# The band mask of local attention: from a TensorE product to a ScalarE copy into PSUM, in five of eight slots

## What is computed

```
sim  = einsum('bhwie,bhwje->bhwij', bq, bk2) * 8
mask = (it < jb) | (it > jb + w) | (jb == -1)
sim  = where(mask, -max, sim)
out  = einsum('bhwij,bhwje->bhwie', softmax(sim), bv2)
```

## Time and profile before

| | |
|---|---|
| median of 3 runs | 3702.38 us (3701.47 to 3703.31) |
| profiled execution: its time, its span | 3697.9 us, 3695.9 us |
| PE busy | 3358.6 us (91%) |
| DVE busy | 2839.3 us (77%) |
| ACT busy | 2300.3 us (62%) |
| POOL busy | 2304.4 us (62%) |
| mean granted clock of TensorE | 0.960 |

### The profile page before, as it was taken

The page is one execution under the profiler, slowest core; times in us unless marked ns, Lnnn a source line. Parts: engine busy times, 40 slices in busy tenths (PEclk is TensorE's granted clock), DMA queues, the critical chain, the costliest instruction groups (busy, mean ns, idle before and its releaser), DMA issues. The chain is left out here.

```text
span 3695.9 us, 150639 instructions
## 1 busy us (share of the span) xinstructions
PE 3358.6 (91%) x64970; PEld 2462.3 (67%) x64970; DVE 2839.3 (77%) x3892; ACT 2300.3 (62%) x4617; POOL 2304.4 (62%) x2078
## 2 busy tenths in 40 slices
PE   7949999999999989999989999999999989999995
PEld 3736667666676666766666666766667666666663
DVE  5348778778878878878878878878878877887783
ACT  4326666666666666666666666666666666666664
POOL 0037666666766666766766766766666666676671
PEclk9769999999999999999999999999999999999997
DMA  1021111111111111111111111101111111111112
GB/s 31 18 75 35 32 30 32 29 30 61 32 30 31 32 30 58 33 32 29 33 29 61 32 29 31 33 28 60 32 29 32 32 29 57 34 32 29 29 32 71
DMA packets 94830, 133.99 MB, mean 36 GB/s; under 512 B 21065, under 2 KB 45152, under 8 KB 93280
## 3 DMA queue, kind: packets, MB, share of 16 engines
q1 hardware_dynamic: 86508, 123.78, 11.3%
q10 hardware_dynamic: 7668, 0.50, 0.2%
HBM read 25.60 MB, written 4.26 MB: 8 GB/s over the span
## 5 line engine op out<-in xcount | busy, mean ns | idle before, releaser
L1032 POOL TENSOR_TENSOR qs<-rprod 128x512 f32<-128x512 f32 x768 | 994.3, 1303 | 669.1 <-DVE rprod L1102 644.3
L1102 DVE TENSOR_TENSOR rprod<-ps,tab 128x1024 f32<-128x1024 f32 x768 | 929.5, 1218 | 284.8 <-PE ps L779 175.6
L1043 POOL TENSOR_TENSOR qs<-qs,rr 128x512 f32<-128x512 f32 x768 | 784.8, 1043 | 281.2 <-ACT rr L964 280.4
L777 PE MATMUL ps<-wh,xls 128*128 128x512 f32 x1152 | 548.3, 476 | 59.4 <-PEq L733 39.9
L828 PEld LDWEIGHTS ps<-pt,v 64*64 64x64 f32 x24768 | 398.6, 135 | 193.6 <-issue 97.0
L788 PE MATMUL ps<-con,qs 128*128 128x128 f32 x3080 | 508.3, 288 | 2.8 <-issue 2.8
L945 ACT ACTIVATE sq<-ps 128x512 f32<-128x512 f32 x384 | 228.6, 595 | 442.6 <-PE ps L779 438.0
L828 PE MATMUL ps<-pt,v 64*64 64x32 f32 x24768 | 442.1, 221 | 66.2 <-ACT pt L954 62.1
L1048 POOL TENSOR_TENSOR pr<-pr,rinv 128x512 f32<-128x512 f32 x386 | 420.1, 1088 | 127.4 <-DVE rinv L1143 127.4
L1121 DVE TENSOR_REDUCE ssq<-sq 128x16 f32<-128x1024 f32 x384 | 464.0, 1208 | 0.0
L779 PE MATMUL ps<-wh,xhs 128*128 128x512 f32 x1152 | 455.9, 396 | 0.0
(11 more groups left out here) (160 smaller groups left out, 5170.2 us busy)
## 6 DMA issues: line engine op xcount, KB each, us to landing
v<-v SPq DMA_DIRECT2D x384, 192.0 KB
v<-v SPq DMA_DIRECT2D x288, 64.0 KB
raw<-in_L_ffn_Wqkv SPq DMA_DIRECT2D x7, 1536.0 KB, 6.4
wo<-in_L_ffn_Wo SPq DMA_DIRECT2D x6, 512.0 KB, 8.6
sT<-so SPq DMA_DIRECT2D x22, 96.0 KB, 1.6
bias<-in_L_attn_hidden_states SPq DMA_DIRECT2D x8, 256.0 KB, 5.5
srow<-sT SPq DMA_DIRECT2D x8, 256.0 KB, 3.2
xrow<-in_L_attn_hidden_states SPq DMA_DIRECT2D x8, 256.0 KB, 4.1
```

The source lines that it names most:

```text
L777: nc.tensor.matmul(dst, al, bh, start=True, stop=False)
L1032: nc.gpsimd.tensor_tensor(qs[:, i % 2, j].rearrange("p (h s d) -> p h s d", s=2, d=HALF), prod[:, 0, j].rearrange("p (h s d) -> p h s d", ...
L1043: nc.gpsimd.tensor_tensor(q3, q3, rr[:, 8 * j:8 * j + 8].unsqueeze(2).broadcast_to([P, 8, DH]), ALU.mult).then_inc(cur["mul"], 1)
L1102: return nc.vector.tensor_tensor(prod[:, :, j, :].rearrange("p c (h d) -> p c h d", d=DH), ps[:, bank, :].rearrange("p (h d) -> p h d", d= ...
```

## The change

In full rounds, for the scores of slots 2 to 6, TensorE no longer forms the mask product. ScalarE copies the mask (bf16 in SBUF) into the score bank at the end of the slot before, that is at the end of slots 1 to 5, behind its copy `kT` and ahead of that slot's extra steps. The new event `mk` tells TensorE that it is there. The score products add to it as before. The scores of slots 7, 0 and 1 keep the product, because the bank SC is used by the feed-forward part between slots 7 and 1.

```diff
-                after(pe, "sub", i)
-                if i == 0 and pb0 is not None:
-                    pe.wait_ge(other["gl"], 3)
-                if i == 1 and pb0 is not None:
-                    pe.wait_ge(cur["h"], 3)
-                nc.tensor.matmul(ps[:, SC, :], identb[:], maskb[:, int(tb > 0), :], start=True, stop=False,
-                                 skip_group_check=True)
+                if full and 2 <= i <= 6:
+                    pe.wait_ge(cur["mk"], i - 1)
+                else:
+                    after(pe, "sub", i)
+                    if i == 0 and pb0 is not None:
+                        pe.wait_ge(other["gl"], 3)
+                    if i == 1 and pb0 is not None:
+                        pe.wait_ge(cur["h"], 3)
+                    nc.tensor.matmul(ps[:, SC, :], identb[:], maskb[:, int(tb > 0), :], start=True, stop=False,
+                                     skip_group_check=True)
                 after(pe, "qte", i)
                 after(pe, "kte", i)
...
+                if full and 1 <= i <= 5:
+                    act.wait_ge(cur["sub"], i + 1)
+                    nc.scalar.copy(ps[:, SC, :], maskb[:, int(unit(i + 1, 2)[1] > 0), :]).then_inc(cur["mk"], 1)
                 if i == 1 and nb is not None:
                     shift_high(nb, 1 - k).then_inc(cur["xh"], 1)
```

More of the change, by code:

```diff
@@ L190 @@
          "woa wo mean var gup aup w2 xh xl fq fr fh gl h x2 x1 fx fc fn fl "
-         "wh wl w1h w1l vc tab shifted cleared").split()
+         "wh wl w1h w1l vc tab mk shifted cleared").split()
 def chunked_attention(nc, t, ctx, sb0, sem0, clear, con, ident, ps, xT, sT):
```

## The result

Over 17 runs of each kernel the changed one takes 3716.46 us (median, 3705.25 to 3737.5) and the one before 3702.33 (3688.94 to 3713.05). The ratio is 1.0038, with a 95% interval of 1.0027 to 1.0049: slower by 10 to 18 us. The profiled execution of the changed kernel took 3705.25 us, with a span of 3703.4 and a mean granted clock of 0.962; 3697.9 and 0.960 stood against it before. Whole executions of one kernel scatter by 24 to 32 us, so most of what follows is read from the inside of a round, where most steps repeat to 0.01 us.

A forecast was written before the change was run, and what follows sets the result against it. TensorE bounds slots 1 to 3, VectorE and POOL slots 4 and 5, ScalarE the second rotation of slot 6. Gains 17.8 us, costs 31.5 us: +13.7 on 3697.9, plus 4.5 to the median: 3716, range 3700 to 3730.

The forecast's parts named there:

- The product is worth 0.22, not 0.31: TensorE's scores: removing a mask product saves 0.22 us; the remaining 0.09 is the switch to small pieces, which stays.
- It pays in slots 2 and 3 only: Plain rounds: removed products gain 0.22 us each in slots 2 and 3, and 0 in slots 4, 5 and 6.
- The reason given for slot 4: Slots 4 and 5: the residual can come earlier, but slot 5's gs still waits for POOL's chain; gain 0.
- Slot 5's copy costs its full length: End of slot 5, plain rounds: the copy stands before the square that times everything, moving the round's gate by 0.50 us.
- Rival 1: End of slot 5: the copy is hidden after all; -1.8 us, 3700.6, no change; chance 0.10.
- rival 3: TensorE's work is the limit throughout: 3650 if all five removed products pay, 3671 if only slots 2 to 4; chance 0.08.
- The copies in slots 1 to 4 of plain rounds are hidden: End of slots 1 to 4: ScalarE waits for TensorE's keys, 1.47 us before slot 5, so copies cost nothing.
- The rounds at a layer's change: new_hf0: two 0.50 us copies, two 0.22 gains; new_hf1: two copies, no gain; new_ff: two copies, slot 2's gain only.
- Copies stand ahead of the first two: 2 x 0.50: new_hf0, 6 rounds: copies ahead of the weight casts of slots 4 and 5, awaited by VectorE, cost 0.50 us each.
- The first round was put at two gains and no cost: First round: two removed products counted as gains of 0.22 us each, with no copy counted as a cost.
- TensorE's wait at slot 6's turn at about 0.95: Slot 6's turn: profile sign that TensorE's idle time, 0.51 us before, becomes about 0.95.
- rival 4: Slots 6 and 7: longer TensorE idling lowers the clock more often; another 8 such rounds make +20 us, 3736; chance 0.12.

The follow-up runs named there:

- e3: Kernel before without the mask products of slots 2 to 6 and without any copy (no mask added there): 3685.16 us, ratio 0.9941.
- e6: Kernel before without the mask product of slot 4 alone, no copy: 3703.47 us, one execution.
- e8: Kernel before without POOL's second copy into fx, so half of fx stays old: 3680.54 us, one execution.
- e9: e3 without POOL's second copy into fx, so half of fx stays old: 3663.05 us, one execution.
- e1: Changed kernel without the copy at the end of slot 5; slot 6 keeps its mask product: 3686.69 us, ratio 0.9948.
- e2: Changed kernel with slot 5's copy moved into slot 6, between the keys' square and the queries' square: 3693.01 us, ratio 0.9966.
- e4: Kernel before with the five copies added and all mask products kept: 3727.86 us, ratio 1.0063.
- e5: Changed kernel with copies only at the end of slots 1 and 2, none in new_hf1 rounds: 3702.85 us, ratio 1.0014; repeated 3701.7 us, ratio 1.0001.
- e12: e5 with a needless copy at the end of slot 5 in all rounds, slot 6 keeping its product: 3734.19 us, ratio 1.009.
- e11: e1 without copies in new_hf1 rounds (copies at the end of slots 1 to 4 elsewhere): 3690.82 us, ratio 0.9968.

## Why the prediction was right

The forecast was 3716, made of +13.7 on 3697.9 and 4.5 of distance to the median; the median is 3716.46.

- *The product is worth 0.22, not 0.31.* Right: 0.64 against 0.42 in the timeline, 0.22 and 0.21 in the slots. The 0.09 of the switch stayed.
- *It pays in slots 2 and 3 only.* Right: e3 for all five. e6 for slot 4 shows it in 20 of 31 rounds in full. The reason given for slot 4, POOL's chain over `fx` to `gs`, is shown by e8 and e9.
- *Slot 5's copy costs its full length.* Right: e1 and e2. The copy was 0.52 start to start, where I had taken 0.50, and e4 had 0.49 for it in the plain round. Rival 1 (hidden after all) is out; so is rival 3.
- *The copies in slots 1 to 4 of plain rounds are hidden.* Right: slots 1 to 4 of e4 are those of before.
- *The rounds at a layer's change.* `new_hf1` was right: +1.02 for 1.00. The term "Copies stand ahead of the first two: 2 x 0.50" was mis-sized, and it is the largest error of the sum. `new_hf0` came out 0.22 us shorter, where 1.00 - 0.44 = +0.56 was forecast, and `new_ff` 0.55 longer instead of 0.78. What I left out is that the work behind the cast was itself slowed by POOL at its old place. A delay of 0.52 in it cost 0.11. The first round was put at two gains and no cost, -0.44; it came out 0.9 us longer (56.66 to 57.56).
- *TensorE's wait at slot 6's turn at about 0.95.* Wrong as put: it is 0.64. Part of its lead is now spent earlier, where the value projection waits for ScalarE's `oT`. From the last of the keys' products to the turn it is 2.03 us (1770.78 to 1772.81), and was 1.60 (1697.83 to 1699.43): 0.43 more, which is the forecast's 0.44. These two rows are of before and of the changed kernel:

```profile
PEld ps L777 <- ACT oT L978: 34.9, 60, 2.0
```

```profile
PEld ps L777 <- ACT oT L981: 77.8, 92, 2.1
```

With the sizes as measured the sum is +9.8 us instead of +13.7. The measured interval is +10 to +18, so this is at its edge. (The range's upper bound was a slip: half of the way from 3716 to rival 4's 3736 is 3726, not 3730. The median lies within either.) Rival 4, the clock, may have the rest of up to 8 us, but I have not shown that: the clock's mean over the changed kernel's 17 runs is 0.960, and so it is over the 17 of before beside e1 to e4. The agreement of 3716 with 3716.46 is therefore luckier than its parts.

## What to carry to other kernels

A unit taken off the busiest engine is worth only what the stretches pay in which that engine times the round: here two of five, and four of five once another engine's chain had been shortened (e9). A unit added to a half idle engine is free or costs its full length, depending on what stands next in its order; two instructions further on it was free. And before a delay is priced at its length, look whether the thing delayed runs slowed by a neighbour at its old place.

## What was not expected of the hardware

- The mean granted clock differs between kernels whose rounds hardly differ: 0.955 and 0.957 (e5, twice) against 0.962 (e1), with the same plain round of 68.61 us. In e5 this ate all that its slots had won. Neither the length of the plain round (e12) nor TensorE's idle time (e1 against e5) foretold it. What does stays open. Of the versions that keep the mask e1 measured lowest, 0.9948, but from six executions, and its interval overlaps with those of e2 and e11; which of the three is best is not shown.
- What a 128x512 operation costs in ScalarE's row goes, in these rows, with where it reads and not with where it writes. End of slot 5 of a `new_hf0` round, changed kernel:

```profile
1346.88 0.59 ACT L987 COPY kT<-ps 128x512 f32<-128x512 f32 x1
1347.36 0.60 ACT L991 CAST ps<-maskb 128x512 f32<-128x512 bf16 x1
1347.88 0.63 ACT L998 CAST wh<-raw 128x512 fp32r<-128x512 f32 x1
1348.40 0.64 ACT L1010 ACTIVATE fq<-fc 128x512 f32<-128x512 f32 x1
1348.93 0.59 ACT L948 ACTIVATE sq<-ps 128x512 f32<-128x512 f32 x1
```

`kT` goes from PSUM to SBUF: 0.48 us start to start. The mask (bf16) goes from SBUF to PSUM: 0.52. `wh` and `fq` go from SBUF to SBUF: 0.52 and 0.53. No experiment changed the source or the destination alone. The Trainium skill (ScalarE: Activation LUTs, "Step-by-step: what each stage is for") says that the way to PSUM is the faster one. Here that shows in the time of one instruction, 603 ns in the mean against 630 for `wh`, but not in the distance from start to start, which is what the copy costs.
